# Two DMA transposes per tile of quantised rows, the first with the upper half, and an order laid out anew, in an eight-head macaron block on one core

## The chip, the core and the metric

The kernel runs on one core of a Trainium2 chip. Its time is the device time of one launch in microseconds, for the whole block; lower is better. The core has the matmul engine TensorE (PE in the profile), VectorE (DVE), ScalarE (ACT), GpSimd (POOL) and the queue of SyncE (SP), which here issues every DMA. The 16 DMA engines of the core move the data.

## What is computed

The input x is 4 batches of 2048 rows of 256 features. The block adds a feed-forward layer with weight 0.5, then differential attention, then the same feed-forward layer again:

```python
x = x + 0.5 * ffn(layernorm(x), w_gate, w_up, w_down)
x = x + attention(layernorm(x), Wq, Wk, Wv, Wproj, lq1, lk1, lq2, lk2)
x = x + 0.5 * ffn(layernorm(x), w_gate, w_up, w_down)

def fp4_quant_dequant(x):                 # blocks of 16 along the last axis
    scale = max(max(abs(block)) / 6, 1e-12)
    return GRID[searchsorted(MID, abs(block / scale))] * sign(block) * scale

def fp4_linear(x, w):
    return fp4_quant_dequant(x) @ fp4_quant_dequant(w).T

def ffn(x, w_gate, w_up, w_down):         # 256 -> 704 -> 256
    h = silu(fp4_linear(x, w_gate)) * fp4_linear(x, w_up)
    return fp4_linear(h, w_down)
```

The attention has 8 heads with two query and key halves of 16 features each and values of 32. q and k get an RMS norm and a rotary embedding, the scores are causal over 2048 keys, each half has its softmax, and the output is `(softmax_1 - lam * softmax_2) @ v`. A layer norm per head, a constant factor and the projection `Wproj` follow.

## The kernel before

The rows lie in 64 tiles of 128 rows, 16 to a batch; four tiles make a chunk (16 chunks), two tiles a pair. The work is cut into stages, each a short run of instructions on one engine for one tile, pair or attention step, and has four passes: the first feed-forward layer (pass 0), the projections to q, k and v (pass 1), the output projection (pass 2) and the second feed-forward layer (pass 3). Attention steps (scores on TensorE, exp on ACT, a mask on POOL where the diagonal crosses, values on TensorE) run between them. Passes of different chunks overlap, so that TensorE does scores and values of one chunk while other engines quantise rows of another.

The order is not written out. `whole_plan` adds the stages with what they need, which ring buffers they take and free, and a due time from the table `DUE`. `Plan.order` starts again and again the stage that can begin first by its own costs (`COST`, `REACH`, `TURNED_X`, `TURNED_H`), and the due time decides between those that could begin at once. The lists that come out are the instruction streams of the five queues; each queue works in its order and waits on semaphores. `WIDE` says for which chunk and head group the scores may hold three pairs of PSUM banks in place of two.

For TensorE a row must lie with its features on the partitions, in 16 bits. A pair of x tiles (256 features each, 512 columns) or one h tile (704 columns) is therefore split into an upper and a lower half in fp16, side by side in `x16` or `h16`: [P, 2, 512] or [P, 2, 704]. `high_x` and `high_h` write the upper half. They run on ACT (L1090) where `cast` holds, that is in passes 1 and 2 and the first three chunks of pass 0, and on POOL (L939, through `half_of`) everywhere else. `low_x` and `low_h` write the lower half on POOL (L1003 or L939). Then the stage `turn_x` or `turn_h` on SP waits for the lower half and for the slot of `xT16` or `hT16` to have been read by TensorE, and one DMA transpose (L921) turns both halves: 8 blocks of 128 columns for x, 11 for h. Its landing lets the matmuls start (`hidden` L1391, `project_qk` and `project_v` L1415, `down` L1404, `project_out` L1466), and frees the one buffer in `x16` or `h16` for the next upper half. The rings: `h16` 1, `hT16` 2, `x16` 2, `xT16` 2, and for passes 1 and 2 rings of their own with 1 buffer each (`p16`, `pT16`). Each tile of q and k is turned by two more DMA transposes on the same queue (L934), behind the wait at L857 that all queues use.

The end of the program is a chain of h tiles of the last chunk: `divide_h` (L956, POOL), square (L1063, ACT), grid and points (L1246 and L1251, DVE), upper and lower half (L939, POOL), transpose, `down`, `add_down` (L1258, DVE), store.

Of the kernel before, what the change touches and what calls it, by code (L numbers as in the profile page):

```python
# [14 lines left out]
P = 128  # L15
# [42 lines left out]
    "add_down0": (-2001134, -273051, -2572070, -2292041, -613124, -186207, 989168, -69482, 3864715, 4757424, 167322, 1059005, -585584, 1226409, -982718, 2217603, -746472, -915550, 2199953, 2698217, 857821, 2305689, 4037657, 4656876, 2030669, 2198860, 822551, 4225067, -1014410, 3297449, 138104, 2844743),  # L58
    "add_down3": (598094, -558718, -1292082, -1504390, -1170731, -2521706, -972593, 1447652, 675773, 5971039, -523567, -2157130, 391691, 2456200, 3802870, 369201, 2868330, 4789025, 4513624, 2376784, 1410949, 641286, 3044792, 2119324, 951173, 1636142, -539924, -1438438, 7385451, 10666683, 7710489, 9517745),
    "add_out": (147495, 1917311, 1680452, 454766, -113886, -650134, 752688, 3136273, -939687, 3111631, -4764622, -2755708, 124072, -816632, 4970533, 2503237, 459305, 4136229, -762874, -1325614, -1676027, -309711, 216717, 610260, -1589184, 2710137, 123954, -1466792, 3680917, 3225387, -2044630, -1226855),  # L60
    "copy_o": (-1153509, 149566, -1314817, -2397141, -2256533, -1445530, -1139776, -314328, 77429, 1189742, 242009, 3318121, 492078, 2190849, -789072, -3101599, 2248601, 1514437, 2402738, -794303, -189455, -3738926, -1150668, -1145827, 789798, 2043086, -1984860, 985384, 1334940, -1603377, 4129389, 7477866),
# [112 lines left out]
LONE = 4  # L174
PAIRS = (0, 2, 4, 5, 1, 3)
PARTS = ((0, 512), (512, 704))
PIECES = ((0, 512), (512, 1024), (1024, 1408))
TANH_OF = {0: PARTS[0], 2: PARTS[1]}
WIDTH = PARTS[-1][1]
HALF = P // 2  # L180
HALVES = 2 * NH * 4 * HD
K_AT = HALVES - HD

TILES_OF = (4, 2)
KTILES = [(lo + i * (hi - lo) // n, (hi - lo) // n) for (lo, hi), n in zip(PARTS, TILES_OF) for i in range(n)]
COST = dict(dequant_h=1385, dequant_x=1058, load=700, store=700, add_down=475, add_out=475, copy_o=680, divide_h=1385,
# [221 lines left out]
def whole_plan():  # L408
# [3 lines left out]
    plan = Plan()  # L412
# [216 lines left out]
def macaron_kernel(nc, x, wq, wk, wv, wproj, lq1, lk1, lq2, lk2, w_gate, w_up, w_down, rope, out):  # L629
# [14 lines left out]
    with ExitStack() as ctx:  # L644
# [247 lines left out]
        def sync_stages(sp, events):  # L892
# [10 lines left out]
            for e in events:  # L903
# [10 lines left out]
                elif e[0] in ("turn_x", "turn_h"):  # L914
# [3 lines left out]
                    if before:  # L918
                        until(sp, "sp", *turned_read(kind, before))
# [996 lines left out]
```

## Time and profile before

| what | value |
| --- | --- |
| time, median of 3 runs | 2073.8 us (2071.68 to 2077.19) |
| the profiled execution | 2066.27 us |
| its span, first to last instruction | 2064.3 us |
| TensorE busy | 1837.9 us, 89% |
| ACT, DVE, POOL busy | 1589.7, 1576.8, 1398.5 us |
| DMA engines | 34.3% of 16 engines' time over the three queues |
| mean granted TensorE clock | 0.983 of full speed |

Busy times say how much of the span an engine worked; they do not say which engine ended a wait. For that the profile has the waits (who waited for whom), a view of one line or tile (how long its instructions took and who waited for it) and the chain of waits that ended last, followed back from the last instruction. A link of that chain that is a DMA runs from the issue on SP to its landing. The profiled execution is 7.5 us below the median of the runs, so differences are taken within the trace and set off against the median.

### The profile page before, as it was taken

How to read it: one execution, taken by the hardware profiler on the slowest of the kernel's cores; microseconds unless marked ns; L12 is line 12 of the kernel's file. 1: busy time of each engine (PE TensorE's matmuls, PEld its weight loads, DVE VectorE, ACT ScalarE, POOL GpSimd, SP SyncE). 2: the span in 40 equal slices, each digit the busy share in tenths (PEclk: the TensorE clock that was granted, in tenths of full speed). 3: DMA queues.
4: the chain of work that ended last, by engine and by line, in shares of the span. 5: the costliest groups of instructions: out<-in, count | busy, mean ns of one | idle time of the engine just before them, and what ended most of it. 6: DMA issues, size and time to landing. Idle time of an engine off the chain costs nothing.

```text
span 2064.3 us, 37249 instructions
## 1 busy us (share of the span) xinstructions
PE 1837.9 (89%) x13634; PEld 782.2 (38%) x13634; DVE 1576.8 (76%) x3782; ACT 1589.7 (77%) x2165; POOL 1398.5 (68%) x1503
## 2 busy tenths in 40 slices
PE   2677999999999899999999799999999899999866
PEld 1343444343334334444433343444443333433233
DVE  8899888888847788898946888897886686642375
ACT  3455888868797897878888798778788889889931
POOL 7789888766645787787844887776875667532254
PEclk9899999999999999999999999999999999999988
DMA  4134445234212345334321445333243333311013
GB/s 130 25 68 90 85 76 90 56 74 88 39 48 42 75 78 103 65 63 88 73 49 30 76 81 86 71 67 68 53 82 61 72 64 76 72 25 25 16 30 73
DMA packets 477478, 136.01 MB, mean 66 GB/s; under 512 B 458224, under 2 KB 477040, under 8 KB 477296
## 3 DMA queue, kind: packets, MB, share of 16 engines
q1 hardware_dynamic: 477296, 133.65, 33.8%
q8 instruction: 107, 1.75, 0.4%
q14 instruction: 75, 0.61, 0.1%
HBM read 11.96 MB, written 8.39 MB: 10 GB/s over the span
## 4 chain that ended last, share of the span: by engine, by line
PE 39%; DVE 21%; ACT 15%; POOL 13%; issue 5%; DMA 3%; SPq 0%; POOLq 0%; DVEq 0%; ACTq 0%
PE psum L1391 11%; ACT probs L1140 11%; PE psum_o L1449 11%; PE psum L1404 6%; PE psum L1430 6%; POOL h L939 3%; DVE psum L1170 2%; PE psum L1415 2%; DVE hq L1246 2%; POOL probs L1040 2%; DVE hq L1251 2%; DMA hT<-h 2%; DMA xT<-x 1%; PE psum L1466 1%; POOL hq L956 1%
## 5 line engine op out<-in xcount | busy, mean ns | idle before, releaser
L1140 ACT ACTIVATE probs<-psum 128x1024 f32<-128x1024 f32 (+2 forms) x1152 | 1055.1, 996 | 139.5 <-PE psum L1430 90.8
L1449 PE MATMUL psum_o<-probs,v_sb 128*32 128x512 f32 (+3 forms) x5120 | 559.1, 537 | 23.4 <-POOL probs L1040 16.0
L1391 PE MATMUL psum<-w_gu_T,xT 128*128 128x512 f16 (+1 forms) x2304 | 504.8, 368 | 50.0 <-DMA xT<-x 16.1
L939 POOL TENSOR_TENSOR h<-hq,qscale 128x704 f16<-128x704 f32 x232 | 328.9, 1435 | 143.8 <-DVE hq L1251 110.2
L1430 PE MATMUL psum<-q_stack,k_stack 64*128 64x512 f16 (+3 forms) x2560 | 366.9, 351 | 57.2 <-ACT probs L1140 46.2
L1391 PEld LDWEIGHTS psum<-w_gu_T,xT 128*128 128x128 f16 x2304 | 213.1, 99 | 325.3 <-issue 63.9
L1404 PE MATMUL psum<-w_down_T,hT 128*128 128x256 f16 x2176 | 265.8, 278 | 28.4 <-DMA hT<-h 19.2
L1430 PEld LDWEIGHTS psum<-q_stack,k_stack 64*128 64x128 f16 x2560 | 94.9, 93 | 425.3 <-ACT probs L1140 281.2
L1040 POOL TENSOR_SCALAR_AFFINE_SELECT probs<-probs 128x512 f32<-128x512 f32 x256 | 169.1, 672 | 126.7 <-ACT probs L1140 126.2
L1404 PEld LDWEIGHTS psum<-w_down_T,hT 128*128 128x128 f16 x2176 | 210.0, 100 | 90.3 <-issue 29.8
L956 POOL TENSOR_TENSOR hq<-hq,rscale 128x704 f32<-128x704 f32 x128 | 184.4, 1441 | 76.5 <-DVE rscale L1179 75.0
L1053 ACT ACTIVATE hq<-psum,tanh_scale 128x512 f32<-128x512 f32 (+1 forms) x256 | 142.4, 559 | 121.7 <-PE psum L1391 117.1
L1449 PEld LDWEIGHTS psum_o<-probs,v_sb 128*32 128x32 f32 x5120 | 119.4, 108 | 267.1 <-issue 172.1
L1246 DVE SCALAR_TENSOR_TENSOR hq<-grid,hq 128x704 f32<-128x704 f32 x128 | 142.8, 1116 | 39.5 <-ACT grid L1063 38.9
L939 POOL TENSOR_TENSOR x<-xq,qscale 128x512 f16<-128x512 f32 x116 | 133.7, 1170 | 44.3 <-DVE xq L1251 44.1
L1415 PE MATMUL psum<-w_qkv_T,xT 128*128 128x512 f16 (+1 forms) x768 | 141.1, 331 | 9.8 <-DMA xT<-x 5.8
L1251 DVE SCALAR_TENSOR_TENSOR hq<-grid,hq 128x704 f32<-128x704 f32 x128 | 145.9, 1140 | 1.0
L1063 ACT ACTIVATE grid<-hq 128x704 f32<-128x704 f32 x128 | 102.0, 797 | 52.7 <-POOL hq L956 36.9
L1003 POOL TENSOR_TENSOR x<-xq,x 128x512 f16<-128x512 f32 x70 | 88.0, 1258 | 59.9 <-ACT x L1090 59.9
L1076 ACT ACTIVATE xq<-xb,offset,rstd 128x256 f32<-128x256 f32 x192 | 104.5, 606 | 22.8 <-POOL offset L982 13.0
L1258 DVE SCALAR_TENSOR_TENSOR xb<-psum,down_scale,xb 128x256 f32<-128x256 f32 x128 | 60.3, 475 | 75.5 <-PE psum L1404 75.1
L1170 DVE TENSOR_REDUCE psum<-hq 128x44 f32<-128x704 f32 x128 | 113.6, 887 | 4.2
(128 smaller groups left out, 2276.3 us busy)
## 6 DMA issues: line engine op xcount, KB each, us to landing
xb<-L_attn_x SPq DMA_DIRECT2D x16, 512.0 KB, 4.0
out<-xb SPq DMA_DIRECT2D x16, 512.0 KB, 3.1
xT<-x SPq DMA_TRANSPOSE x128, 3.1
hT<-h SPq DMA_TRANSPOSE x128, 3.5
k_stack<-st SPq DMA_TRANSPOSE x64, 2.9
q_stack<-st SPq DMA_TRANSPOSE x64, 3.3
k_stack<-L_ffn_w_down SPq DMA_DIRECT2D x1, 704.0 KB, 4.0
k_stack<-L_ffn_w_gate SPq DMA_DIRECT2D x1, 512.0 KB, 5.4
```

The costliest lines, as they stand in the source:

```text
L939: return nc.gpsimd.tensor_tensor(by_block(halves(kind, key)[:, n, :]), by_block(buffers(kind, key)[0]), scale.unsqueeze(2).broadcast_to([P ...
L956: nc.gpsimd.tensor_tensor(by_block(a), by_block(a), rscale[:, i, 0:nb].unsqueeze(2).broadcast_to([P, nb, QB]), ALU.mult).then_inc(scaled_r ...
L1040: nc.gpsimd.affine_select(out=blk, in_=blk, compare_op=ALU.is_ge, fill=0.0, base=0, pattern=[[0, 4], [1, P]], channel_multiplier=-1)\
L1140: nc.scalar.activation(to, src, ACT.Exp, scale=HD ** -0.5 / QK_SCALE ** 2)\
L1170: nc.vector.tensor_reduce(am, by_block(src), AX_X, ALU.max, apply_absolute_value=True)\
L1246: nc.vector.scalar_tensor_tensor(a, g, GRID_BASE, a, ALU.add, ALU.add).then_inc(grid_ready, 1)
L1251: nc.vector.scalar_tensor_tensor(a, g, GRID_BASE, a, ALU.add, ALU.subtract)\
L1391: last = nc.tensor.matmul(bank(e)[:, 0:hi - lo], xs[:, x, t % 2, k, :], w_gu_T[:, w, k, lo:hi], start=n == 0, stop=n == len(parts) - 1)
L1404: last = nc.tensor.matmul(bank(e)[:, 0:C], hs[0:n, k, :], w_down_T[0:n, w, :], start=i == 0, stop=i == len(parts) - 1)
L1415: last = nc.tensor.matmul(bank(e)[:, 0:hi - lo], xs[:, x, t % 2, k, :], w_qkv_T[:, w, k, lo:hi], start=n == 0, stop=n == len(parts) - 1)
L1430: last = nc.tensor.matmul(psum[:, plan.pairs[s, u] + j, first:first + w], k_stack[half, at, h, kt % NTC * P:(kt % NTC + 1) * P], q_stack[h ...
L1449: last = nc.tensor.matmul(psum_o[at:at + VD, q0:CHUNK], v_sb[:, kt // NTC % SLOTS * NTC + kt % NTC, 2 * g + u, :], probs[:, s % 3, 2 * u + ...
```

## The change

Each transpose of x or h becomes two. A new stage `send_x` or `send_h` on SP waits for the upper half and for the slot to be free, and turns the first 4 blocks (x) or the first 5 (h, which all lie in the upper half of 704 columns). `turn_x` or `turn_h` waits for the lower half and turns the other 4 or 6. The landing semaphore now counts 32 for a tile. On POOL the upper half signals a new semaphore, `upper_ready`. Two needs are new: in pass 1 the norm and the upper half of an x pair come after those of the pair before it, across chunks too. The planner's costs for the stages and the tables `DUE` and `WIDE` have other numbers.

```diff
 DUE = {
...
-    "load": (122595, 122595, 151687, 151687, -249324, -249324, 126250, 126250, -10280, -10280, 305179, 305179, -724145, -724145, 719117, 719117, -1486225, -1486225, 1038334, 1038334, -259650, -259650, 1213902, 1213902, 547298, 547298, 955524, 955524, 239902, 239902, 2928996, 2928996),
+    "load": (122595, 122595, 151687, 151687, -249324, -249324, 126250, 126250, -10280, -10280, 267632, 267632, -1740209, -1740209, 905540, 905540, -257785, -257785, 1490175, 1490175, -423181, -423181, 1967132, 1967132, 942332, 942332, 692363, 692363, -123382, -123382, 3293562, 3293562),
...
-WIDE = {0: (0, 2, 4, 5, 9, 10, 12, 14, 15), 1: (1, 3, 7, 11, 14, 15), 2: (0, 3, 6, 7, 11, 12, 13, 14, 15), 3: (0, 2, 3, 4, 7, 8, 10, 11, 14, 15)}
+WIDE = {0: (1, 3, 4, 6, 8, 9, 12, 13, 15), 1: (2, 3, 5, 7, 8, 10, 11, 13, 14, 15), 2: (2, 3, 6, 7, 8, 10, 11, 12, 13, 14, 15), 3: (0, 2, 3, 5, 7, 11, 14, 15)}
...
+SENT = dict(x=4, h=5)
...
-            square_x=620, stats=1820, tanh=690, transpose_o=470, turn_x=1250, turn_h=1400, turn_qk=2700)
+            square_x=620, stats=1820, tanh=690, transpose_o=470, turn_x=1060, turn_h=1160, send_x=1060, send_h=1110, turn_qk=2700)
...
-TURNED_X, TURNED_H, TURNED_QK = 2200, 2400, 2200
+TURNED_X, TURNED_H, TURNED_QK = 1800, 2000, 2200
...
+    def sent(kind, *key):
+
+        u = (kind, *key)
+        at = lambda stage: (of_pair if kind == "x" else of_tile)(stage + kind, *key)
+        half, turned = rings_of(*key)[1:] if kind == "x" else ("h16", "hT16")
+        lands = TURNED_X if kind == "x" else TURNED_H
+        add(("send_" + kind, *u), "sync", at("send_"), [("high_" + kind, *u)], [(turned, key)], lands=lands)
+        add(("turn_" + kind, *u), "sync", at("turn_"), [("low_" + kind, *u), ("send_" + kind, *u)], [], [(half, key)],
+            lands=lands)
...
-        add(("high_x", *u), "scalar", of_pair("high_x", pas, p), [made], [(rings_of(pas, p)[1], (pas, p))])
+        add(("high_x", *u), "scalar", of_pair("high_x", pas, p), [made, ("high_x", "x", 1, p - 1) if pas == 1 and p else None], [(rings_of(pas, p)[1], (pas, p))])
...
-                add(norm, "scalar", of_pair("norm_a", *pair), [("rstd", 1, c), ("norm_a", "x", 1, pair[1] - 1) if i else None,
+                add(norm, "scalar", of_pair("norm_a", *pair), [("rstd", 1, c), ("norm_a", "x", 1, pair[1] - 1) if pair[1] else None,
...
-                16 * (plan.ring[r][key] // plan.sizes[r] + 1)
+                32 * (plan.ring[r][key] // plan.sizes[r] + 1)
...
-                elif e[0] in ("turn_x", "turn_h"):
+                elif e[0] in ("send_x", "send_h", "turn_x", "turn_h"):
                     kind, key = e[1], e[2:]
-                    until(sp, "sp", low_ready, LOW["low_" + kind, *e[1:]] + 1)
-                    before, n = before_in(ring(kind, key, 2), key), slot_of(kind, key, 2)
-                    if before:
-                        until(sp, "sp", *turned_read(kind, before))
+                    n, whole = slot_of(kind, key, 2), halves(kind, key).rearrange("p s f -> p (s f)")
                     to = xT16[:, n].rearrange("p s i k t -> p (s i k) t") if kind == "x" else hT16[:, n]
-                    sp.dma_start_transpose(to, halves(kind, key).rearrange("p s f -> p (s f)"))\
-                        .then_inc(landed(kind, key)[0], 16)
+                    split = SENT[kind]
+                    if e[0][:4] == "send":
+                        if cast(kind, *key):
+                            until(sp, "sp", high_ready, HIGH["high_" + kind, *e[1:]] + 1)
+                        else:
+                            until(sp, "sp", upper_ready, UPPER["high_" + kind, *e[1:]] + 1)
+                        before = before_in(ring(kind, key, 2), key)
+                        if before:
+                            until(sp, "sp", *turned_read(kind, before))
+                        to, src = to[:, 0:split, :], whole[:, 0:split * P]
+                    else:
+                        until(sp, "sp", low_ready, LOW["low_" + kind, *e[1:]] + 1)
+                        to, src = to[:, split:, :], whole[:, split * P:]
+                    sp.dma_start_transpose(to, src).then_inc(landed(kind, key)[0], 16)
...
-                    half_of(kind, key, 0)
+                    half_of(kind, key, 0).then_inc(upper_ready, 1)
```

What stands in a row on SP, first in the third batch, about 1152 to 1168 us in the trace: `xT<-x` and `hT<-h` are the transposes of x pairs and h tiles with their blocks, `k_stack<-st` and `q_stack<-st` those of a tile of k and q. Before:

```order
203 L934 DMA_TRANSPOSE k_stack<-st 128x8x128
204 L934 DMA_TRANSPOSE q_stack<-st 128x8x128
205 L921 DMA_TRANSPOSE xT<-x 128x8x128
206 L934 DMA_TRANSPOSE k_stack<-st 128x8x128
207 L934 DMA_TRANSPOSE q_stack<-st 128x8x128
208 L934 DMA_TRANSPOSE k_stack<-st 128x8x128
209 L934 DMA_TRANSPOSE q_stack<-st 128x8x128
210 L921 DMA_TRANSPOSE xT<-x 128x8x128
211 L921 DMA_TRANSPOSE hT<-h 128x11x128
212 L934 DMA_TRANSPOSE k_stack<-st 128x8x128
213 L934 DMA_TRANSPOSE q_stack<-st 128x8x128
```

In the changed kernel the same four tiles of k and q stand so:

```order
298 L960 DMA_TRANSPOSE k_stack<-st 128x8x128
299 L960 DMA_TRANSPOSE q_stack<-st 128x8x128
300 L960 DMA_TRANSPOSE k_stack<-st 128x8x128
301 L960 DMA_TRANSPOSE q_stack<-st 128x8x128
302 L948 DMA_TRANSPOSE xT<-x 128x4x128 x2
303 L948 DMA_TRANSPOSE hT<-h 128x5x128
304 L948 DMA_TRANSPOSE hT<-h 128x6x128
305 L960 DMA_TRANSPOSE k_stack<-st 128x8x128
306 L960 DMA_TRANSPOSE q_stack<-st 128x8x128
307 L960 DMA_TRANSPOSE k_stack<-st 128x8x128
308 L960 DMA_TRANSPOSE q_stack<-st 128x8x128
```

The first x pair moved from behind one tile of k and q to behind two, and an h tile moved in ahead of the last two.

POOL at the very end of the program: `hq<-hq,rscale` is `divide_h`, and each `h<-hq,qscale x2` is the upper and the lower half of one h tile. Before:

```order
1164 L956 TENSOR_TENSOR hq<-hq,rscale 128x704
1165 L939 TENSOR_TENSOR h<-hq,qscale 128x704 x2
1166 L956 TENSOR_TENSOR hq<-hq,rscale 128x704
1167 L939 TENSOR_TENSOR h<-hq,qscale 128x704 x2
1168 L956 TENSOR_TENSOR hq<-hq,rscale 128x704
1169 L939 TENSOR_TENSOR h<-hq,qscale 128x704 x2
1170 L956 TENSOR_TENSOR hq<-hq,rscale 128x704
1171 L939 TENSOR_TENSOR h<-hq,qscale 128x704 x2
```

After:

```order
1155 L982 TENSOR_TENSOR hq<-hq,rscale 128x704
1156 L965 TENSOR_TENSOR h<-hq,qscale 128x704 x2
1157 L982 TENSOR_TENSOR hq<-hq,rscale 128x704 x2
1158 L965 TENSOR_TENSOR h<-hq,qscale 128x704 x2
1159 L982 TENSOR_TENSOR hq<-hq,rscale 128x704
1160 L965 TENSOR_TENSOR h<-hq,qscale 128x704 x4
```

Two divides are drawn ahead, so that the halves of the last two tiles follow one another. SP's end in the changed kernel, which has all h pieces in turn behind the last but one store:

```order
514 L925 DMA out<-xb 128x4x256
515 L948 DMA_TRANSPOSE hT<-h 128x5x128
516 L948 DMA_TRANSPOSE hT<-h 128x6x128
517 L948 DMA_TRANSPOSE hT<-h 128x5x128
518 L948 DMA_TRANSPOSE hT<-h 128x6x128
519 L948 DMA_TRANSPOSE hT<-h 128x5x128
520 L948 DMA_TRANSPOSE hT<-h 128x6x128
521 L925 DMA out<-xb 128x4x256
```

Before, three whole h transposes stood between the same two stores; each now is a piece of 5 blocks and a piece of 6.

## Rows read from the trace of the kernel before

**Rows 1.** The page: busy time and share, then TensorE's busy tenths in 40 slices.
```profile
PE 1837.9 (89%) x13634; PEld 782.2 (38%) x13634; DVE 1576.8 (76%) x3782; ACT 1589.7 (77%) x2165; POOL 1398.5 (68%) x1503
...
PE   2677999999999899999999799999999899999866
```

**Rows 2.** View of line 921: issue ns min/median/max, then who waited for it (us, times).
```profile
L921 SPq DMA_TRANSPOSE xT<-x x128: 1231/1233/2393, 43.5 to 2019.2; - x128
L921 SPq DMA_TRANSPOSE hT<-h x128: 1262/1383/2517, 81.2 to 2053.1; - x128
...
  POOL h L939: 33.5, 19
  PE psum L1404: 19.2, 11
  PE psum L1391: 16.1, 5
  PE psum L1415: 5.8, 4
  PE psum L1466: 5.7, 3
```

**Rows 3.** The chain that ended last, from several stretches: start us, us, link.
```profile
90.35 3.33 DMA xT<-x
...
242.72 5.27 DMA hT<-h
...
384.59 4.61 DMA xT<-x
...
668.43 4.24 DMA xT<-x
...
690.43 3.21 DMA xT<-x
...
1041.70 4.65 DMA hT<-h
...
1308.04 4.91 DMA hT<-h
...
1546.57 3.70 DMA hT<-h
...
2011.48 3.09 DMA xT<-x
...
2046.28 3.52 DMA hT<-h
...
2053.10 3.53 DMA hT<-h
```

**Rows 4.** The page's DMA issues: count, median us from issue to landing.
```profile
xT<-x SPq DMA_TRANSPOSE x128, 3.1
hT<-h SPq DMA_TRANSPOSE x128, 3.5
```

**Rows 5.** Stretches of 1 us after an isolated h transpose; last columns: clock, DMA share, GB/s.
```profile
82.00:83.00 1.00, 1.00 (x4) 0.41 (x3) 0.94 (x2) 0.43 (x1) 1.00 (x2) 0.50 0.59 118
83.00:84.00 1.00, 1.00 (x4) 0.30 (x2) 0.60 (x1) 0.88 (x2) 1.00 (x2) 0.54 1.11 209
84.00:85.00 1.00, 1.00 (x6) 0.49 (x5) 1.00 (x3) 0.68 (x2) 1.00 (x1) 1.00 0.18 34
```

**Rows 6.** The page's groups of POOL's halves: busy us, mean ns of one, idle before.
```profile
L939 POOL TENSOR_TENSOR h<-hq,qscale 128x704 f16<-128x704 f32 x232 | 328.9, 1435 | 143.8 <-DVE hq L1251 110.2
...
L1003 POOL TENSOR_TENSOR x<-xq,x 128x512 f16<-128x512 f32 x70 | 88.0, 1258 | 59.9 <-ACT x L1090 59.9
```

**Rows 7.** SP's issues in order of time, at two places: start us, us.
```profile
241.44 1.23 SPq L921 DMA_TRANSPOSE xT<-x  x1
...
1162.41 1.30 SPq L934 DMA_TRANSPOSE q_stack<-st  x1
1163.80 1.28 SPq L921 DMA_TRANSPOSE xT<-x  x1
```

**Rows 8.** SP's own waits: us in total, times, longest us.
```profile
SPq L857 <- PE psum L1415: 70.1, 11, 9.6
```

More of the change, by code:

```diff
@@ new lines @@
+    "project_v": (-1428176, 1481917, -1041866, 2592229, 2392064, 1691251, -192212, 650539, -1332303, 2319095, 1145437, 2602535, 1832694, 4991618, -755034, -1607096, 196959, 2690819, 1167755, 1834260, 2030341, 4136048, 3075228, 1247107, 3357728, 4314019, 265599, 611463, 3168202, 2801561, -2078041, 82721),
+    "quant_h0": (-2048423, 28945, -1780780, -2558018, 1808595, 1158575, 1727187, 3145494, 4981965, 5077054, -3005691, -682345, -304696, 1954812, -997369, -56741, -107651, -181488, 1603551, 3962432, -549943, 821042, 2591731, 3936676, 4232425, 1187272, 2134803, 2387278, -1678209, 410273, 2960769, 3472283),
@@ new lines @@
+    "quant_h3": (931100, 81241, 1664297, -2328413, -1659952, -1815833, -2269024, 1641248, -1185745, 837117, -1210004, -207977, 953992, 1710095, 3909245, 1482269, 2780362, 2612951, 5835154, 3052927, -2267754, -1557148, 4911882, 3359897, 5729055, 5417363, 7393463, 7045299, 6328484, 8531401, 7347212, 10420645),
+    "read_qk": (-2411914, -477661, 1763560, 3310415, 120251, -480761, -475809, 20318, -2022356, -278571, -125035, 2581561, -637959, 3086419, 3463139, 1087543, 3047327, 3390460, 5053693, 4031564, 2364364, 5750409, 2802569, 4751013, 3228798, 4363746, -585052, 743029, 1609704, 535012, -284604, 3306961),
@@ new lines @@
+    "read_v": (-1306473, 1951645, 2020876, 2539182, 1671224, 63171, 206453, 1221620, 1148207, 2753278, -1371066, 44682, 1917823, 6289717, -126712, 459671, 1612615, 4093404, 1326326, 3813358, 2664364, 3910932, 2110026, 3974293, 983696, 2950063, -1189820, -466840, 3086111, 1366050, -1045889, -36793),
+    "rms": (33351, 2855326, -317045, 1143914, 1948340, 1231778, 188420, -329996, -12818, 1934869, -3272203, -1381394, 2274928, 4213280, -833287, -2051867, 2278183, 2973780, 2175531, 2689864, 2845250, 4500294, -931742, -675526, 4331762, 5084183, -1630264, -553105, 86856, -1090125, -776469, 741734),
@@ new lines @@
+    "tanh0": (-1523377, 546441, -1427324, -768620, 352397, -1001807, 1280806, 2342477, -432726, -497559, -3083596, -1463121, -1043636, 2452079, -1367886, 360739, 904195, -1178203, 2103542, 927178, -88085, 780170, 1629474, 1623687, 2438631, 501947, 872866, 2800333, 276807, -362735, 512246, 2959354),
+    "tanh3": (1465301, 2555543, -256897, -2356668, -4010270, -3761996, -2893529, 195567, -4727483, -384683, 383794, -192601, -497574, 170980, 3617469, -247528, 3110481, 3083567, 5941420, 2845307, 275624, 652272, 6146152, 3476835, 8220314, 6871141, -135381, -899578, 14113495, 15609406, 2672318, 5111155),
@@ new lines @@
+    "transpose_o": (-406665, -1576783, 175176, -863085, 1063889, 515613, -3510438, -1269192, -1125328, 1741016, 2536041, 2735038, -2701947, -668722, 1705984, -2320511, 2156362, 360374, 90994, -1322144, 2720457, 1211514, 6010868, 4899648, 3600502, 1316963, 4003920, 1853231, -1895588, -5961945, 914914, 6074576),
+    "turn_h0": (-1428753, 1158105, -532961, -857553, 622674, -392242, -11559, 245833, 1798341, 4413099, -2770321, 649846, -1507900, 97154, -964938, 859047, -534220, -385129, 30985, 1502303, 1414391, 1523512, -57441, 427952, 4176323, 2425530, 2448627, 4585466, 1359049, 432996, 790829, 3094235),
@@ L210 @@
 PORT_LEAD = 140
[L211 to L214 removed]
+TURNED_X, TURNED_H, TURNED_QK = 1800, 2000, 2200
+X_STAGES = ("norm_a", "scale_x", "divide_x", "square_x", "grid_x", "points_x", "dequant_x", "high_x", "send_x", "low_x", "turn_x")
 LEAD = {("stats", 0, 0), ("rstd", 0, 0), *((stage, "x", 0, p) for stage in X_STAGES for p in range(NTC // 2))}
@@ L427, in of_tile @@
         return kind + str(pas), t // NTC, t % NTC, NTC - 1
+    def sent(kind, *key):
[6 more added lines that the diff above has]
+            lands=lands)
     def halved(pas, p, made):
         u = ("x", pas, p)
-        add(("high_x", *u), "scalar", of_pair("high_x", pas, p), [made], [(rings_of(pas, p)[1], (pas, p))])
+        add(("high_x", *u), "scalar", of_pair("high_x", pas, p), [made, ("high_x", "x", 1, p - 1) if pas == 1 and p else None], [(rings_of(pas, p)[1], (pas, p))])
         add(("low_x", *u), "gpsimd", of_pair("low_x", pas, p), [("high_x", *u)], [], [(rings_of(pas, p)[0], (pas, p))])
-        add(("turn_x", *u), "sync", of_pair("turn_x", pas, p), [("low_x", *u)], [(rings_of(pas, p)[2], (pas, p))],
-            [(rings_of(pas, p)[1], (pas, p))], lands=TURNED_X)
+        sent("x", pas, p)
     def quantise(kind, key, needs, takes, frees):
@@ L466, in quantise @@
             [(own, key)], weight=weight)
-        add(("turn_" + kind, *u), "sync", at("turn_" + kind), [("low_" + kind, *u)], [(turned, key)], [(half, key)],
-            lands=TURNED_X if kind == "x" else TURNED_H)
+        sent(kind, *key)
     def mlp(pas, tiles, stats):
@@ L742, in macaron_kernel @@
         points_ready = sem("points_ready")
+        upper_ready = sem("upper_ready")
         quantised = sem("quantised")
@@ L782, in macaron_kernel @@
         HIGH = ordinals(order["scalar"], ("high_x", "high_h"))
+        UPPER = ordinals(order["gpsimd"], ("high_x", "high_h"))
         LOW = ordinals(order["gpsimd"], ("low_x", "low_h"))
```

51 lines of the change are left out of this document (20 added, 31 removed), and 138 rows, old and new, of the table DUE.

## The prediction

> **What bounds the kernel now.** I read the busy line and the slices first [rows 1]. TensorE is busy 89% of 2064.3 us, so it stands idle for 226 us; the slices are at 9 or over except at the start, at about 600 to 700 us, 1100 to 1200 and 1600 to 1700 (the seams between batches) and in the last 100 us. DVE, ACT and POOL are at 68 to 77%, so no one of them is the bound over the whole span. The time is set by chains that run through all engines where TensorE has nothing ready. Next, who waited for the turned rows [rows 2]: TensorE 46.8 us in 23 waits (16.1 + 19.2 + 5.8 + 5.7), POOL 33.5 us in 19, all of the latter for `h16`, of which there is one buffer. Third, the chain that ended last [rows 3]: 16 transposes of x and h rows stand on it, some 61 us, 3% of the span. That is what the change works on. The profiled execution took 2066.27 us, of which 2064.3 are the span; the median of the runs shown is 2073.8, 7.5 us more. I work out a difference in the trace and take it off the median.
>
> **A piece of half the size.** Before, one DMA turns 8 blocks of 128 x 128 for an x pair, or 11 for an h tile, once the lower half is written. After, blocks 0 to 3 (x) or 0 to 4 (h) go when the upper half is there, and only 4 or 6 blocks are left to go with the lower half. An x transpose lands 3.1 us from issue, an h transpose 3.5 [rows 4]: 0.4 us for 3 blocks more, 0.133 us a block. By that row the last piece lands 4 x 0.133 = 0.53 us earlier for x and 5 x 0.133 = 0.67 us earlier for h. The other bound comes from the 16 DMA engines during an isolated h transpose [rows 5]: 0.59 + 1.11 + 0.18 = 1.88 us of their time for 11 blocks, 0.171 a block, and 0.05 a block in the issue on SP (1383 less 1233 ns over 3 blocks, [rows 2]); 0.22 together, or 0.88 us for x and 1.1 for h. On the other side the gain can be nothing, or a loss of one issue, if SP is still issuing the first piece when the lower half is ready. I take 0.53 and 0.67, since the landing rows measure the very thing. The first piece is covered by the step that makes the lower half: on POOL that takes 1435 ns for h and 1258 for x on average [rows 6], against an issue of 1233 - 4 x 50 = 1033 ns for the x piece and 1383 - 6 x 50 = 1083 for the h piece. If that cover is gone (the queue reaches the first piece late), the second piece starts up to one issue late and loses up to 1.08 us, more than it won.
>
> **What of it lies on the path.** Of the 16 links, two x transposes stand at the start and two at the end, and two h transposes at the end [rows 3]; nothing else is there to take their place, for TensorE sits idle beside them. They give 4 x 0.53 + 2 x 0.67 = 3.5 us. In the tail SP has one kind of work left, as its order shows: pieces of x and h alone. The last two h links hang together through the single `h16`: POOL may write the next upper half only when both pieces have landed, so both count in full. Of the ten links in the middle, five are plain (3.21 to 3.70 us; two x, three h): 2 x 0.53 + 3 x 0.67 = 3.1 us. The other five are long (5.27, 4.61, 4.24, 4.65, 4.91): the first, for one, was issued right behind an x transpose that SP began at 241.44 [rows 7], so part of such a link is queueing, which a shorter piece does not take away. There I count 0.4 us each, 2.0 us, with 0 and 0.67 as the ends. Together 3.5 + 3.1 + 2.0 = 8.6 us. At the upper bound of the piece all 16 links would give 8 x 0.88 + 8 x 1.1 = 15.8 us; if the middle has a second path as long as this one, which TensorE's many slices of 9 make possible, only the 3.5 us of the two ends stay.
>
> **What SP pays.** Before, its transposes take 128 x 1.233 + 128 x 1.383 + 128 for q and k at about 1.28 = 499 us, 24% of the span. After, 256 x 1.033 + 128 x 1.083 + 128 x 1.133 + 164 = 711 us, 34%. A queue at 34% is no bound, but it serves in order. Near 1160 us an x turn starts only at 1163.80, right behind a q transpose that was issued at 1162.41 [rows 7]. The new wait is also earlier: the first piece must find its slot in `xT16` or `hT16` read by TensorE, and what is queued behind it on SP are the q and k transposes, on which the scores of the next chunk wait. In the part of the order shown for this place, two groups of q and k now run ahead of the x pieces where one did before. I put one more issue, about 1 us, on the path in total (bounds 0 and the rival below).
>
> **The new order and the two chained stages.** The table moves instructions on all engines, but the work is the same: the same matmuls, and the rows left on POOL for the last tiles are the same divides and halves with two divides drawn ahead. Neither the start nor the tail shows a wait removed by it. The two chained stages (norm and upper half of pass 1 now in order across chunks) add no instruction; they cost something only where a later pair would have been ready first. The changed widths of the scores ring move no instruction's cost either. I take 0 for all of this, with 8 us on either side; that is about one and a half of the longest transpose links, and a small share of the 226 us in which TensorE is idle.
>
> Sum: -8.6 + 1.0 + 0 = -7.6 us. That is 2058.7 for the profiled execution and 2073.8 - 7.6 = 2066.2 against the median; I say 2066.
>
> **The rivals.**
> *The gain is taken back (same).* The transposes in the middle had slack through another engine. For it: TensorE waited for x or h rows on 46.8 us only, and in the seams POOL and DVE chains run beside them. Against it: POOL's 19 waits for `h16` shorten too. It leaves 3.5 us at the ends, less 1 to 3 us for SP, so -2 us or so: 2072, and with the order 2068 to 2078.
> *SP's queue becomes the hold-up (slower).* The place is the turn of q and k at each chunk's end. If one more piece stands ahead of it, or waits there for its slot, in each of the 16 chunks, that is 16 x 1.083 = 17.3 us on the path; less 8.6 us of gain it ends at +8.7, 2082 to 2083. It decides from the point where more than 8 of the 16 chunks see it (8 x 1.083 = 8.7 us is the gain). For it: SP already waits at the slot check for TensorE's reading of the v projection 70.1 us in 11 waits [rows 8], and that check now comes earlier. Against it: most q and k turns wait for POOL and not for the queue, and SP rests two thirds of the time. The Trainium skill, in DMA: Bandwidth & Descriptors, Rules for kernel authors, says to coalesce many small transfers into one large one; by that rule two DMAs for one are the wrong way round. The trace agrees in part: 1.233 us of issue for 8 blocks at 0.05 a block leaves 0.83 that each piece pays anew.
> *The order makes a hole (slower).* One wait of 8 us or more at a seam that the old order did not have; 2074 to 2080 after the gain. Nothing in the rows points to a place.
> *The change does not do what it says.* The first piece could go out no earlier than the second, when high and low parts are written back to back and SP is late; both pieces then go together. The landing would be as before plus an issue. That is the mechanism of the SP rival on the ends as well, and I give it no chance of its own.
>
> **How the numbers follow.** My forecast, shorter links with the middle at least half kept, has 0.50; the same-case has 0.28; SP's queue 0.13; a hole from the order 0.09. A difference of 0.3% (6.2 us) is about what a measurement of this kernel can tell from no change, so faster means below 2067.6 and slower above 2080.0. The forecast's own range runs from 2054 (the upper bound of the piece, 15.8 us, and some 4 us from the order) to 2068. Nearly all of that is faster: 0.49, and with a small part of the same-case 0.51. Of the slower rivals three quarters lie above 2080, 0.17; same is what is left, 0.32. To hold 8 in 10 the range goes from 2054 to 2081.
>
> **What would show it right or wrong.** In the profile after, the last x pieces should land in about 2.6 us and the h pieces in 2.8, with issues near 1.03 and 1.13 us. TensorE's waits for x and h rows should fall from 46.8 to about 35 us, and POOL's for `h16` from 33.5 to about 21. The last two h links should be near 2.85 us each in place of 3.52. DMA packets stay the same in number. If the waits fall but the span does not, it is the same-case; if SP shows many first pieces waiting on TensorE with q and k behind them, and TensorE's wait for q and k turns rises from almost nothing, it is the SP rival. Wrong at the root would be an issue that does not shrink with the blocks (1.23 us each), or a landing that stays at 3.1.

## The result

The changed kernel took 2083.7 us (median of five runs, 2081.43 to 2086.68) against 2073.8 us before (five runs, 2071.68 to 2077.19). The ratio is 1.0046 with a 95% interval of 1.0036 to 1.0057: it is slower by 9.9 us, where 7.6 us less were forecast, and 2083.7 lies above the range. The profiled execution took 2083.03 us, its span is 2081.3 us.

The page of the changed kernel, busy line and TensorE's slices, answers to [rows 1]:

```profile
PE 1849.3 (89%) x13634; PEld 780.8 (38%) x13634; DVE 1588.9 (76%) x3782; ACT 1592.7 (77%) x2165; POOL 1399.0 (67%) x1503
...
PE   2677999899998899999999899999999889999866
```

TensorE is idle for 232.0 us (226.4 before) and busy for 11.4 us more, with the same 13634 matmuls. So of the 17.0 us between the two profiled spans (one execution of each kernel, further apart than the medians) 5.6 are idle time, and in 11.4 the same number of matmuls took longer. The granted clock was 0.983 before and is 0.978 now. At 100 to 200 us (us, busy us and count of PE, PEld, DVE, ACT, POOL, clock, DMA share, GB/s), before and then after, 429 matmuls are busy for 3.5 us more at the lower clock, though they need not be the same 429:

```profile
100.00:200.00 100.00, 73.27 (x429) 39.24 (x430) 93.49 (x189) 53.46 (x87) 89.28 (x78) 0.97 0.39 76
```

```profile
100.00:200.00 100.00, 76.77 (x429) 39.26 (x427) 89.94 (x186) 53.58 (x86) 86.68 (x80) 0.92 0.37 73
```

What brought the clock down was not tested: the delays described below may have done it, or the new order.

No slice stands out. The loss is spread: the 8th, 13th and 33rd slices (52 us each) are at 8 and were at 9, and the 23rd, the seam at 1150 us, is better than it was.

The view of the line that issues the pieces (ns min/median/max, then who waited, us and times) answers to [rows 2]:

```profile
L948 SPq DMA_TRANSPOSE xT<-x x256: 1188/1256/2747, 40.2 to 2033.6; - x128
L948 SPq DMA_TRANSPOSE hT<-h x256: 1199/1210/2426, 80.4 to 2069.7; - x128
...
  POOL h L965: 38.1, 17
  PE psum L1417: 18.0, 10
  PE psum L1430: 15.8, 11
  ACT x L1116: 15.7, 16
  PE psum L1492: 7.3, 7
  PE psum L1441: 4.3, 7
```

A piece of 4 blocks holds SP for 1.256 us (median; 1.191 for the first pieces alone, 1.264 for the second ones), the whole of 8 blocks held it for 1.233. The issue did not shrink. SP's transposes take 256 x 1.256 + 256 x 1.210 + 64 x (1.252 + 1.310) = 795 us, 38% of the span; 499 us before, 711 forecast. TensorE's waits for the rows add up to 45.4 us in 35 waits (46.8 in 23 before), POOL's for `h16` grew from 33.5 to 38.1, and a waiter is new: ACT, which waits 15.7 us in 16 waits to write an upper half into the one buffer `p16` (3.1 us in 3 waits before); that buffer comes free when the last piece has landed.

The landing did get shorter, as the page's issues show [rows 4]:

```profile
xT<-x SPq DMA_TRANSPOSE x256, 2.5
hT<-h SPq DMA_TRANSPOSE x256, 2.7
```

The chain that ended last (start us, us, link), at two places; it is followed back over the last 600 us only. In all of the chain of before [rows 3], issues of x and h stood for 0.43 us in one link. Now seven of them stand in this last part alone, with 8.45 us:

```profile
1567.99 1.07 POOL x L965
1569.06 0.02 issue
1569.08 1.20 SPq L948
1570.28 0.04 issue
1570.33 4.02 DMA xT<-x
1574.35 0.05 issue
1574.39 1.47 PE psum L1417 x6
...
1620.77 1.43 PE psum L1441 x12
1622.20 0.02 issue
1622.22 0.02 SPq L874
1622.23 0.03 issue
1622.26 1.19 SPq L948
1623.45 0.04 issue
1623.50 3.69 DMA xT<-x
```

And POOL at the first of these places:

```profile
1567.99 2.08 POOL L965 TENSOR_TENSOR x<-xq,qscale 128x512 f16<-128x512 f32 x2 [3.18 <-DVE xq L1277]
```

Two halves in 2.08 us: the lower one is written by 1570.07, but SP issues the first piece until 1570.28 and starts the second at 1570.33. At the second place neither half ends the wait. SP waited for the slot, until TensorE had read it (L1441), and both pieces go one behind the other: the second starts 1.24 us later than one whole DMA would.

That is the arithmetic of the loss. Where SP can only start when both halves are there, before needs 3.1 us for x and 3.5 for h. After, the second piece starts 1.24 us (x) or 1.25 us (h) behind the first: 1.24 + 2.5 = 3.74 for x and 1.25 + 2.7 = 3.95 for h, 0.5 to 0.6 us more, and SP is held twice as long.

How often that is so I counted in the traces, with each piece paired with its own halves by the order of the stages. The last DMA of an x pair starts more than 0.1 us behind its lower half in 57 of 128 pairs before and in 107 of 128 after; the median delay goes from 0.03 to 1.85 us. (An expectation below has 1.27 for the latter, which this pairing does not bear out.) In 78 of the 107 the first piece was itself more than 0.1 us late behind its upper half, so that both go late together; in 29 it went at once, and only its issue stood in front of the second. For h it is 34 of 128 after and 17 before, and the median delay is 0.03 us in both. Many second h pieces do follow their first within 0.15 us, 82 of 128, but 60 of these start 0.03 us behind their lower half, as they would have without a first piece. Part of the delay for x is a wait for the slot, which both kernels have.

What it comes to, from the end of the lower half to the landed rows (median us over 128): x 3.55 before and 4.51 after, h 3.56 and 2.77. The x rows arrive 1.0 us later, though each DMA is 0.6 us shorter.

The tail's links did what was forecast. They answer to the last three of [rows 3], which took 3.09, 3.52 and 3.53 us:

```profile
2027.50 2.43 DMA xT<-x
...
2064.05 2.73 DMA hT<-h
...
2069.67 2.73 DMA hT<-h
```

The last exp (L1140 before, L1166 after, on ACT) ends at 1967.9 us before and at 1985.5 after, so 17.6 us of the profiled executions are lost before the tail. The stretch behind it takes 96.5 us before and 95.8 after: of the 2.4 us that its four shorter links were to give, less than 1 us is seen.

### The profile page after: what moved, and what is told of

The parts are those of the page before. It is cut to its first block and busy times, and to the rows that moved or that the text cites. A ratio compares the mean times of both kernels' runs of the same rounds, so it can differ in the third digit from the quotient of the medians.

```text
span 2081.3 us, 37501 instructions
## 1 busy us (share of the span) xinstructions
PE 1849.3 (89%) x13634; PEld 780.8 (38%) x13634; DVE 1588.9 (76%) x3782; ACT 1592.7 (77%) x2165; POOL 1399.0 (67%) x1503
## 2 busy tenths in 40 slices
DMA packets 485673, 136.08 MB, mean 65 GB/s; under 512 B 466416, under 2 KB 485232, under 8 KB 485488
## 5 line engine op out<-in xcount | busy, mean ns | idle before, releaser
L1166 ACT ACTIVATE probs<-psum 128x1024 f32<-128x1024 f32 (+2 forms) x1152 | 1054.4, 1003 | 125.4 <-PE psum L1456 85.9
L1456 PE MATMUL psum<-q_stack,k_stack 64*128 64x512 f16 (+3 forms) x2560 | 372.4, 351 | 61.5 <-ACT probs L1166 48.4
L1456 PEld LDWEIGHTS psum<-q_stack,k_stack 64*128 64x128 f16 x2560 | 95.8, 93 | 448.8 <-ACT probs L1166 318.3
L1272 DVE SCALAR_TENSOR_TENSOR hq<-grid,hq 128x704 f32<-128x704 f32 x128 | 155.8, 1217 | 24.5 <-ACT grid L1089 23.9
L1441 PE MATMUL psum<-w_qkv_T,xT 128*128 128x512 f16 (+1 forms) x768 | 141.9, 329 | 18.6 <-DVE qscale L1210 6.4
L965 POOL TENSOR_TENSOR x<-xq,qscale 128x512 f16<-128x512 f32 x116 | 129.3, 1134 | 36.8 <-DVE xq L1277 33.7
L1277 DVE SCALAR_TENSOR_TENSOR hq<-grid,hq 128x704 f32<-128x704 f32 x128 | 147.8, 1155 | 0.7
L1249 DVE SCALAR_TENSOR_TENSOR hq<-hq,psum 128x512 f32<-128x512 f32 x128 | 86.8, 678 | 45.5 <-ACT hq L1079 45.0
```

What stands on the lines that cost most here:

```text
L965: return nc.gpsimd.tensor_tensor(by_block(halves(kind, key)[:, n, :]), by_block(buffers(kind, key)[0]), scale.unsqueeze(2).broadcast_to([P ...
L1166: nc.scalar.activation(to, src, ACT.Exp, scale=HD ** -0.5 / QK_SCALE ** 2)\
L1272: nc.vector.scalar_tensor_tensor(a, g, GRID_BASE, a, ALU.add, ALU.add).then_inc(grid_ready, 1)
L1277: nc.vector.scalar_tensor_tensor(a, g, GRID_BASE, a, ALU.add, ALU.subtract)\
L1441: last = nc.tensor.matmul(bank(e)[:, 0:hi - lo], xs[:, x, t % 2, k, :], w_qkv_T[:, w, k, lo:hi], start=n == 0, stop=n == len(parts) - 1)
L1456: last = nc.tensor.matmul(psum[:, plan.pairs[s, u] + j, first:first + w], k_stack[half, at, h, kt % NTC * P:(kt % NTC + 1) * P], q_stack[h ...
```

## Experiments

The theory after the result: an issue that costs SP 1.2 us whatever its size takes back more than the shorter landing gives. The rival: the new order is what costs, and the pieces are innocent. To vary the time of an issue, all the experiments move the rows (those of q and k too) by plain copies in place of the transposes, with the same blocks, semaphores and places in the order, and the same number of buffers; the blocks in `xT16` and `hT16` lie 16 columns further apart. What they leave out is the turning of the rows, in every kernel of this section; TensorE multiplies unturned rows of the same shape. The changed code and the old order with real transposes in another combination were not tried, so the attribution below is that of the copies. That it holds for the transposes is inferred from the same delays in their traces. Ratios are to the kernel before, with its transposes, on the same chip.

```diff
-        hT16 = sb("hT16", [P, HT16, 2 * KD + 1, P], F16)
+        hT16 = sb("hT16", [P, HT16, 2 * KD + 1, P + 16], F16)[:, :, :, 0:P]
...
-                    sp.dma_start_transpose(to, src).then_inc(landed(kind, key)[0], 16)
+                    moved(sp, to, src).then_inc(landed(kind, key)[0], 16)
...
+            return sp.dma_start(to, src.rearrange("p (n t) -> p n t", t=P))
```

Such a copy holds SP for 0.59 us ("quick"). For the other level ("held") a DMA of one element stands behind every copy, so that SP is held for about 1.25 us (0.65 + 0.60, and 1.33 from start to start):

```diff
+            sp.dma_start(to, src.rearrange("p (n t) -> p n t", t=P)).then_inc(done, by)
+            sp.dma_start(spill[idle[0] % P:idle[0] % P + 1, idle[0] // P:idle[0] // P + 1], ident[0:1, 0:1]).then_inc(spilled, 16)
```

The kernels, quick, with the copy's line for the two-piece one in before's order (ns min/median/max):

```profile
L948 SPq DMA_DIRECT2D xT<-x x256: 593/594/1878, 40.0 to 2014.9; - x128
L948 SPq DMA_DIRECT2D hT<-h x256: 593/594/1353, 79.3 to 2048.7; - x128
...
  POOL h L953: 21.4, 12
  PE psum L1418: 12.7, 5
  PE psum L1405: 11.7, 5
```

and held, the same kernel with the one-element DMAs:

```profile
L949 SPq DMA_DIRECT2D xT<-x x256: 649/656/883, 40.0 to 2044.3; - x128
L949 SPq DMA_DIRECT2D hT<-h x256: 649/656/964, 79.4 to 2077.7; - x128
...
  POOL h L956: 36.9, 18
  PE psum L1421: 21.7, 14
  PE psum L1408: 15.2, 6
  ACT x L1107: 9.3, 9
```

Copies land much like the transposes: whole, 2.9 us for x and 3.3 for h; in pieces, 2.3 and 2.4 to 2.6.

| order | DMAs per tile | quick: us, ratio | held: us, ratio |
| --- | --- | --- | --- |
| before's | one | 2066.1, 0.9969; again 2065.5, 0.9960 | 2067.5, 0.9970; again 2065.4, 0.9958 |
| before's | two | 2061.5, 0.9933; again 2062.5, 0.9945 | 2086.7, 1.0067 |
| new | one | 2077.1, 1.0008 | 2075.7, 1.0012 |
| new | two | 2067.7, 0.9972 | 2075.7, 1.0014 |

The intervals are 0.0012 to 0.0026 to either side, and each difference below has the scatter of both. Held, from the first row to the last it is +0.0050 with the mean of the two first ones (0.9964): 10 us, as the real kernels had (+0.0046). Quick, it is +0.0008, under 2 us. So among the copies the time of an issue decides the loss.

The delay of the rows goes the same way. From the end of the lower half to the landed rows, and how many of 128 last DMAs start more than 0.1 us behind the lower half, for one DMA and for two in before's order (`copy_before2`, `copy_old_order_two`, `slow_issue_before`, `slow_issue_old_order_two`):

| queue | x: median us | x: late | h: median us | h: late |
| --- | --- | --- | --- | --- |
| quick | 3.18, then 2.85 | 46, then 61 | 3.38, then 2.62 | 12, then 21 |
| held | 3.28, then 3.67 | 57, then 110 | 3.44, then 2.75 | 18, then 41 |

With a quick queue two pieces bring x in earlier, with a held one later. h comes in earlier on either.

**The ends: both kernels, quick and held.** `copy_before2`, `copy_after2`, `slow_issue_before`, `slow_issue_after`.

> The kernel before with every DMA transpose replaced by a plain DMA copy of the same blocks from the same buffer to the same buffer, in rows of 256 bytes: the rows are not turned, so the output is another, but every stage, order, wait and buffer is as before. Expected: the copies issue and land faster than the transposes (1.2 us and 3.1 or 3.5 us), so some 5 to 30 us under the kernel before, 2045 to 2070. It is the base for the other runs with copies.

> The changed kernel with its transposes replaced by plain copies in the same way (rows not turned). Against the same replacement in the kernel before. Order theory (the new order costs the 9.9 us): the gap stays, this is 6 to 14 us slower than the kernel before with copies. Pieces theory (the second issue of 1.2 us on SP costs it): with copies, which issue faster, the gap shrinks to under 4 us or turns round.

> The kernel before with copies in place of transposes (rows not turned, so another output), and behind every copy a second DMA of one element on SP, so that a copy holds SP for about 1.24 us as a transpose does (0.594 us for a copy alone). Issue theory (SP's time per DMA is what costs): a few us over the copies alone (2066.1), since SP goes from some 12% to 24%: 2066 to 2074. Order theory: the same, it says nothing here.

> The changed kernel with copies and the same second DMA of one element behind each (rows not turned): 640 copies hold SP for about 1.24 us each. Issue theory: the 10 us between the two kernels, which copies alone had shrunk to 1.7, come back: 7 to 13 us over the kernel before with the same second DMA. Rival (the transposes' own work in the DMA engines, packets and landing, costs it and not SP's issue): the gap stays under 4 us.

Measured 2066.08 (0.9956 to 0.9981), 2067.74 (0.9958 to 0.9986), 2067.52 (0.9959 to 0.9981) and 2075.7 us (1.0 to 1.0028). Whole DMAs don't mind the held queue; two pieces in the new order lose 8 us by it. Register additions on SP ahead of the copies (`copy_before_padded2`, 2063.65 us in one run) left the issue at 0.594 us, so that kernel tells nothing.

**Two pieces in before's order, held.** The piece of the stage `send` is issued right ahead of its `turn`, inside the old stage:

```diff
+                    until(sp, "sp", upper_ready, UPPER["high_" + kind, *e[1:]] + 1)
...
+                    moved(sp, to[:, 0:split, :], whole[:, 0:split * P], landed(kind, key)[0], 16)
+                    until(sp, "sp", low_ready, LOW["low_" + kind, *e[1:]] + 1)
+                    moved(sp, to[:, split:, :], whole[:, split * P:], landed(kind, key)[0], 16)
```

> The order of the kernel before on every queue, but two pieces for every x and h tile, next to each other on SP, with copies and the second DMA of one element (rows not turned). Issue theory: pieces cost by themselves, 4 to 13 us over the kernel before with the same second DMA. Order theory (with slow issues it is the new order that loses): 0 to 5 us under it, by the shorter landing of the last piece.

Measured 2086.67 us (1.0041 to 1.0093), 21 us above one DMA. ACT's waits for `p16` go from 3.1 to 9.3 us and POOL's for `h16` from 30.9 to 36.9, as in the changed kernel.

**The same, quick.**

> Before's order and table, each x pair and h tile moved in two adjacent pieces, as in slow_issue_old_order_two (2086.7 us), but by plain copies that hold SP for 0.59 us each and no one-element DMA behind them (rows not turned). Theory SP's issue time: what costs is that every piece holds SP's queue for 1.2 us; with 0.59 us the gap to copy_before2 (2066.1) is small: 2064 to 2071. Rival, the split itself (more waits in a row on SP, landings counted together, more DMAs under way): the 19 us stay, 2080 to 2087.

> copy_old_order_two once more, beside copy_before_again on one chip, since the gain of two pieces with a quick queue (2061.5 against 2066.1, ratio 0.9933 against 0.9969) was read across two calls. If the gain of the split is real: 3 to 8 us below copy_before_again. If it was scatter: within 1.5 us of it.

> copy_before2 once more (before with plain copies in place of the transposes, whole tiles): a ratio of 0.996 to 0.998.

Measured 2061.47 (0.9915 to 0.9951), and side by side 2062.48 (0.993 to 0.996) against 2065.49 (0.9947 to 0.9973). Two pieces gain 3.0 us side by side and 7.5 by the ratios of the first measurements, and 7.5 in the new order (1.0008 against 0.9972); the two intervals of the side-by-side runs overlap, so the size is rough. TensorE's waits for rows fall from 41.1 (23.7 + 17.4) to 32.1 us and POOL's for `h16` from 28.4 to 21.4: what was forecast for the real kernel (35 and 21) is what the quick queue gives. Here a pair that SP takes up late costs 0.59 + 2.3 = 2.9 us against 2.9: nothing is lost.

**The new order with one DMA.** The stage `send` issues nothing, and `turn` moves the whole tile:

```diff
+                    if e[0][:4] == "send":
+                        continue
```

> The order of the changed kernel on every queue, but one whole copy per x or h tile where the second piece stood, and the second DMA of one element (rows not turned). Issue theory: without the 256 extra issues the loss is gone, within 4 us of the kernel before with the same second DMA. Order theory: 8 us or more over it.

> The new order, each x pair and h tile moved by one plain copy where the second piece stood (0.6 us on SP, rows not turned). Theory SP's issue time: the new order is no worse when SP is quick: 2063 to 2069, beside 2067.7 of copy_after2. Rival, the new order costs 8 us by itself on whatever queue: 2073 to 2077, as slow_issue_new_order_one had.

Measured 2075.7 (1.0 to 1.0025) held and 2077.14 us (0.9996 to 1.002) quick. My expectation for the second, 2063 to 2069, was wrong: the new order costs 8 to 11 us against before's when the DMAs are whole, on either queue. With two pieces it costs 5 to 8 us quick, and it is 11 us better than before's order held (1.0014 against 1.0067). So the order suits held pieces, and it pays for that with something else. That is hardly idle time: from `copy_before2` to `copy_new_order_one` TensorE's idle time stays (224.5 and 224.2 us), and the same matmuls are busy for 1851.3 us in place of 1835.2; held, idle is 222.4 and 223.0 and busy 1844.2 and 1851.5. The mean granted clock of these four is 0.985 and 0.979, 0.980 and 0.978. The sizes are rough: the repeat of `copy_before2` was idle for 220.0 and busy for 1842.9 us at 0.981. Two held pieces in before's order do cost idle time (237.9 us). Whether the new order costs by way of the clock was not tested. The windows (us, busy us and count of PE, PEld, DVE, ACT, POOL, clock, DMA share, GB/s) show where; `copy_before2`, then `copy_new_order_one`:

```profile
200.00:300.00 100.00, 95.41 (x763) 44.40 (x759) 87.94 (x222) 83.72 (x120) 84.76 (x96) 1.00 0.38 87
300.00:600.00 300.00, 286.16 (x2148) 118.38 (x2146) 234.48 (x565) 247.23 (x326) 204.29 (x223) 1.00 0.27 67
600.00:1000.00 400.00, 374.74 (x2833) 159.83 (x2829) 335.92 (x833) 326.38 (x453) 296.17 (x320) 1.00 0.29 72
```

```profile
200.00:300.00 100.00, 94.71 (x743) 45.34 (x734) 85.65 (x208) 76.07 (x108) 79.74 (x90) 0.97 0.29 70
300.00:600.00 300.00, 284.22 (x2111) 115.33 (x2114) 227.64 (x557) 252.49 (x336) 202.34 (x213) 1.00 0.28 68
600.00:1000.00 400.00, 375.18 (x2830) 159.53 (x2829) 333.19 (x817) 321.46 (x442) 290.23 (x316) 1.00 0.28 70
```

ACT does 7.7 us less at 200 to 300 us, 5.3 more at 300 to 600 and 4.9 less at 600 to 1000; with the 1.5 us it is behind before 200 us, it stands some 9 us behind at 1000. In the real kernels it is 12 us behind there, with the same pattern. Which moved stages do it is not known.

**One piece held, the other quick.** From `slow_issue_old_order_two`, without the one-element DMA behind the first pieces, or without it behind the second ones:

```diff
-                    moved(sp, to[:, 0:split, :], whole[:, 0:split * P], landed(kind, key)[0], 16)
+                    moved(sp, to[:, 0:split, :], whole[:, 0:split * P], landed(kind, key)[0], 16, False)
```

> slow_issue_old_order_two (2086.7 us) without the one-element DMA behind the first pieces: these hold SP for 0.6 us, the second pieces and the tiles of q and k 1.2 as there. Theory, the second piece of the same tile is held up by the first: the first pieces carry most of the 25 us between copy_old_order_two (2061.5) and slow_issue_old_order_two: 2062 to 2069. Rival, SP is merely fuller and every issue counts alike: 256 of the 384 to 448 held issues remain, so some 8 to 12 us are left of the 25: 2073 to 2080.

> The converse: the one-element DMA stands behind the first pieces and behind q and k, not behind the second pieces. Theory, the first piece's issue holds up the second: nearly as slow as slow_issue_old_order_two, 2080 to 2087. Rival, every issue counts alike: the same as slow_issue_first_quick. A third case, the second piece's issue holds up the next tile's: this one near 2065 and slow_issue_first_quick near 2085.

Measured 2064.57 (0.9952, 0.9935 to 0.9968) and 2073.35 us (0.9994, 0.998 to 1.0007). Without the hold behind the first piece the loss is gone. Without the hold behind the second it is more than halved, not kept as my theory had it and not gone as the rival had it. Last x pieces that start more than 0.1 us behind their lower half are 110 of 128 with both held, 99 with the first held, 70 with the first quick and 61 with both quick (h: 41, 35, 32, 21); so the first piece's issue does stand in front of the second, and is the larger part; but the second's hold adds to it, and the two together cost more (1.0067) than the sum over `copy_old_order_two` (0.9939): 0.0013 + 0.0055 = 0.0068 of 0.0128.

**x alone, h alone, in two pieces, held.** In before's order, with the other kind whole:

```diff
+                    if kind != "x":
+                        moved(sp, to, whole, landed(kind, key)[0], 16)
+                        continue
```

> Before's order, copies with a one-element DMA behind each, x pairs in two adjacent pieces and h tiles whole: 128 more pieces on SP where slow_issue_old_order_two had 256 (2086.7 us) and slow_issue_before none (2067.5). If each extra issue costs alike, about half of the 19 us: 2074 to 2080. If only h counts, through the one buffer h16 and POOL: 2066 to 2070. If only x counts, through ACT's upper halves in the one buffer p16: 2083 to 2088.

> Before's order with slow copies, h tiles in two adjacent pieces and x pairs whole. slow_issue_old_order_x_two had 2081.4 (ratio to before 0.0058 above slow_issue_before, some 12 us). If the two parts add up to the 20 us of slow_issue_old_order_two: 8 us above slow_issue_before, 2073 to 2079. If h gains by itself, because its second piece starts mostly on time (median 0.03 us behind its lower half in the changed kernel, x 1.27 us): 2060 to 2067, and a kernel that splits h alone would be the better one.

> slow_issue_old_order_h_two once more, in one call with slow_issue_before and in more rounds, since 2064.8 against 2067.5 is near what can be told apart. If splitting h alone gains with a held queue: a ratio of 0.994 to 0.9965, below slow_issue_before_again by 3 to 6 us. If it was scatter: equal within 1.5 us.

> slow_issue_before once more (x pairs and h tiles whole, a one-element DMA behind every copy): a ratio of 0.996 to 0.998.

x alone: 2081.35 us (1.0028, 1.0014 to 1.0042), 13 us above one DMA. h alone: 2064.8 (0.9951, 0.9934 to 0.9967), and again 2065.8 (0.9959, 0.9946 to 0.9973) beside 2065.42 for one DMA. The gain of the first measurement was scatter; h in two pieces gains nothing and loses nothing that can be measured. x pays: its lower half takes 1.06 us (median of the 58 whose upper half is POOL's) or 1.16 (the 70 of ACT), less than the 1.24 us from the first issue to the second, while a lower half of h takes 1.39 us. Both together lose 21 us and not 13, so the parts don't add up here either.

**The changed code, laid out by before's tables, held.** `DUE` and `WIDE` are those of before, and the first pieces take the due times of the whole transposes; the code, the chained stages and the planner's costs are the new ones.

> The changed code (two pieces with stages of their own, the two chained needs, the new costs of the planner) laid out by the tables DUE and WIDE of before, with the slow copies. If the new tables are what makes it slower than slow_issue_before (2067.5): 2066 to 2071. If the pieces are, and the tables were fitted to soften them: 2078 to 2092, above slow_issue_after (2075.7).

Measured 2196.58 us (1.0585, 1.0557 to 1.0613), above all expectations. A table that was not fitted to its code costs 120 us more than the fitted one, so a comparison of orders says little on its own about what stands in them.

## Why the prediction was wrong

**What bounds the kernel, and the landing: right.** Counted from its own issue, a piece lands 0.6 us (x) and 0.8 us (h) earlier; 0.53 and 0.67 were taken. The last links are 2.73 us for h (2.85 forecast). The DMA packets stayed nearly the same in number (477478 and 485673).

**The issue on SP: the step that failed.** "1233 - 4 x 50 = 1033" drew a line through 8 blocks (1.233 us) and 11 blocks (1.383) and followed it down to 4. The pieces of 4, 5 and 6 blocks took 1.19 to 1.26 us: the line is flat from 4 to 8 blocks. Two rows can't tell a slope from a step, and the line was extended outside them. The text named this as what would be wrong at the root. SP got 296 us more to issue, not 212 (and the terms of that sum add up to 712 us, where the text has 711).

**The cover: wrong with it.** It was taken as 1258 ns for x against 1033, a margin of 0.2 us. 1258 is the mean of the 70 lower halves of L1003; their median is 1.16 us, and the other 58, which are among L939's, have 1.06. From the first issue to the second it is 1.24 us: a deficit of 0.1 to 0.2 us. For h, 1.39 against 1.25 still covers, and h alone lost nothing. The text had the price for lost cover ("up to one issue late and loses up to 1.08 us, more than it won") and gave it no share of the 128 pairs; it should have, since SP's waits for a slot [rows 8] are places where both pieces go late, and in the kernel before the one x transpose was already late in 57 of 128 pairs.

**What of it lies on the path: the gain was too large, the cost far too small.** 8.6 us forecast, 3 to 7.5 in the quick runs. The held queue turned that into a loss of 21 us in before's order, and took back 8 us in the new one. "One more issue, about 1 us" was the mis-sized term: from quick to held, two pieces lose 8 us in the new order (2067.7 to 2075.7) and 24 to 25 in before's (2061.5 and 2062.5 to 2086.7), where whole DMAs lose nothing that can be measured.

**The new order: 0 forecast, with 8 us on either side.** It costs 5 to 11 us where the queue is quick or the DMAs are whole, and saves 11 with held pieces. By one path through the held row: two pieces +21, the new order -11, together +10. By the other: the new order +10, the second piece 0. Both end at the measured 9.9; which part is "the" cause depends on the path, and they should not be read as separate terms. That the order's loss with whole DMAs (8 to 11 us) is near the measured 9.9 is no proof that the order alone is the cause: without the held pieces the new kernel is within 2 us of before (0.9972 against 0.9964).

**The rivals.** SP's queue as the hold-up was the right side and almost the right number (2082 to 2083 us, chance 0.13), but not by the place it named, so the number was luck. TensorE waited for turned q 0.7 us before and 1.4 after, and ACT's `st` waits went from 1.6 to 5.0 us: the turns of q and k are not what is late. It is x, behind its own first piece, and ACT and POOL, which wait for the single buffers `p16` and `h16`. The last rival of the text had the mechanism, both pieces going together "as before plus an issue"; it was given no chance of its own, and 78 of the 128 x pairs do it. The part of the issue that each piece pays anew, 0.83 us in the text, is all of its 1.2. The rule cited from the Trainium skill (DMA: Bandwidth & Descriptors, Rules for kernel authors), that one large transfer is better than many small ones, would have given the right sign here; with a quick queue the same split gained 3 to 7.5 us.

## What to carry to other kernels

Before a DMA is split to start earlier, measure what the smaller DMA holds its queue for, at that very size; if it is the same as the whole, the piece must be covered by a step that is longer than the issue, on nearly all tiles, and every tile that the queue takes up late loses an issue less the shorter landing (here 1.24 - 0.6 us). Split only where the row of that step shows the margin (h here, at best), and count single buffers on the source as waiters. A due-time table and the code it was fitted to are one thing: new code under the old table took 2196.6 us, 120 us more, far above the change under test. TensorE's busy time moved with the order too (by 11.4 us here, with the granted clock from 0.983 to 0.978), so read busy and idle time apart.

## What the runs showed of the hardware

A DMA transpose's issue took 1.19 to 1.26 us (medians 1.256 for 4 blocks, 1.210 for 5 and 6, 1.233 for 8) for 4 to 8 blocks of 128 x 128 and 1.38 for 11; a plain copy of the same blocks took 0.59 us, in pieces or whole, and landed in nearly the same time (2.3 to 3.3 us against 2.5 to 3.5). With whole tiles, doubling the time of an issue cost nothing that could be measured (2066.1 and 2065.5 us against 2067.5 and 2065.4): 384 DMAs of 1.33 us each, a quarter of the span, were free; 640 of them, two fifths, were not (2086.7 us in before's order).
